# T1 written centred with its mean in a 129th column, z on ScalarE with one pointer

## The reference

```python
x = einsum('oc,bchw->bohw', inv(I - circulant(ricker(width, damp))), x)   # mixes the 128 channels
t = x as tokens                                                           # (16, 1024, 128)
n = layernorm(t)
Q, K, V = elu(n @ Wq.T) + 1, elu(n @ Wk.T) + 1, n @ Wv.T                  # 8 heads of 16
t = t + (causal linear attention of Q, K, V) @ W_out.T                    # call this t1
z = layernorm(t1)
g = mean over tokens of (relu(z @ gfc1.T + b) @ gfc2.T + b)               # one gate vector per batch
W1m, b1m, W2m, b2m = W1 + sum_e g[e] * tv_W1[e], ...                      # weights merged per batch
r = z + relu(z @ W1m.T + b1m) @ W2m.T + b2m
t = t1 + layernorm(r) * gain + bias                                       # t1 comes back here
```

## Time and profile before

| | us |
|---|---|
| runs | 747.09, 748.32, 747.53 |
| profiled execution, its own time | 749.55 |
| its span in the trace | 747.80 |
| TensorE busy | 692.5 (93%) |
| VectorE busy | 659.1 (88%) |
| ScalarE busy | 649.1 (87%) |
| GpSimd busy | 465.2 (62%) |

### The profile page before, as it was taken

How to read it: one execution, slowest core, us unless ns; L and a number is a source line. 1 busy time by engine, 2 the same in 40 slices (tenths; PEclk the granted TensorE clock), 3 DMA queues, 4 the chain that set the end, 5 groups by cost and what they waited for, 6 DMA issues and landing times. The chain is left out here.

```text
span 747.8 us, 38168 instructions
## 1 busy us (share of the span) xinstructions
PE 692.5 (93%) x12002; PEld 533.8 (71%) x12002; DVE 659.1 (88%) x2409; ACT 649.1 (87%) x1780; POOL 465.2 (62%) x790
## 2 busy tenths in 40 slices
PE   4898899999999999999999999888999998999993
PEld 2576677777777777777777777775777787777772
DVE  5697889999999999999999999768898977998983
ACT  4797989999999999999999999557888876888883
POOL 3686778888888888888888888421333321333333
PEclk9798999999999999999999999899999999999998
DMA  4757676666666666666666666410222211222221
GB/s 149 112 110 134 132 129 129 148 143 131 148 142 132 148 141 132 148 141 134 148 139 135 148 142 123 74 51 1 73 85 83 71 58 31 85 70 84 84 84 70
DMA packets 202485, 82.66 MB, mean 111 GB/s; under 512 B 176093, under 2 KB 189824, under 8 KB 202377
## 3 DMA queue, kind: packets, MB, share of 16 engines
q1 hardware_dynamic: 202440, 82.08, 48.3%
HBM read 22.79 MB, written 17.30 MB: 54 GB/s over the span
## 5 line engine op out<-in xcount | busy, mean ns | idle before, releaser
L892 DVE SCALAR_TENSOR_TENSOR scores_lo<-p_a,scores_hi 128x512 f16<-128x512 f32 x256 | 173.3, 683 | 1.7 <-ACT scores_hi L786 1.3
L786 ACT ACTIVATE scores_hi<-p_a 128x512 f16<-128x512 f32 x256 | 156.2, 611 | 9.3 <-PE p_a L623 9.3
L1010 POOL CAST qk_parts<-qk_f 128x512 f16<-128x512 f32 x128 | 78.0, 610 | 50.2 <-issue 24.9
L1442 POOL TENSOR_TENSOR ffn_rstd_shift<-ffn_rstd_shift,consts 128x4 f32<-128x4 f32 x32 | 36.5, 1142 | 109.1 <-DVE ffn_rstd_shift L1400 109.1
L984 POOL TENSOR_TENSOR stats<-stats,consts 128x2 f32<-128x2 f32 (+1 forms) x128 | 88.2, 689 | 17.9 <-DVE stats L925 13.1
L1224 PE MATMUL psb<-merged_W_of_batch,h_hi 128*128 128x128 f16 x512 | 94.5, 220 | 2.2 <-DVE h_lo L1378 1.5
L1378 DVE TENSOR_TENSOR h_lo<-h_f,h_hi 128x512 f16<-128x512 f32 x128 | 95.6, 786 | 1.1 <-ACT h_hi L1280 1.1
L1269 ACT ACTIVATE h_f<-psb,merged_b_of_batch 128x512 f32<-128x512 f32 x128 | 87.2, 709 | 10.3 <-PE psb L1205 8.6
L1225 PE MATMUL psb<-merged_W_of_batch,h_hi 128*128 128x128 f16 x512 | 94.2, 220 | 0.0
L1226 PE MATMUL psb<-merged_W_of_batch,h_lo 128*128 128x128 f16 x512 | 94.1, 220 | 0.0
L1016 POOL TENSOR_TENSOR qk_parts<-qk_f,qk_parts 128x256 f16<-128x256 f32 x128 | 85.9, 671 | 10.2
(11 more groups left out here) (215 smaller groups left out, 2697.5 us busy)
## 6 DMA issues: line engine op xcount, KB each, us to landing
x_f<-in_x SPq DMA_DIRECT2D x32, 256.0 KB, 3.2
t_rows<-t SPq DMA_DIRECT2D x64, 128.0 KB, 1.8
t_back<-t_rows SPq DMA_DIRECT2D x32, 256.0 KB, 2.6
out<-out_tile SPq DMA_DIRECT2D x32, 256.0 KB, 2.1
tv_share<-in_L_ffn_tv_W SPq DMA_DIRECT2D x32, 128.0 KB, 2.2
qkT_parts<-qk_parts SPq DMA_TRANSPOSE x128, 3.1
zT_hi_lo<-z_parts SPq DMA_TRANSPOSE x128, 2.3
merged_W<-in_L_ffn_W SPq DMA_DIRECT2D x2, 256.0 KB, 4.4
```

The lines of the kernel that those rows point to most:

```text
L786: nc.scalar.activation(ah[:, t % 2, cols], p_a[:, cols], ACT.Relu).then_inc(ahi_ready[eo], 1)
L892: nc.vector.scalar_tensor_tensor(al[:, t % 2, cols], p_a[:, cols], 0.0, ah[:, t % 2, cols], ALU.max, ALU.subtract).then_inc(alo_ready[eo], 1)
```

## The change

The weights that make t1 are centred, so that t1 comes out of `out_project` with mean 0 over the channels: block 4 of `w_in` is now the centred mix, and `w_outT` has each row's mean taken off. The mean itself comes out as one more column, the 129th, of the same four matmuls. `read_t1` copies 129 columns, the stores and loads carry them. `normalise` now is a copy with one pointer, z = t1 times one over the deviation; `shift2` is gone. In the second phase `add_up` puts the mean back: instead of one addition over 512 columns it is four scalar_tensor_tensor instructions of 128 columns, each adding t1 and the mean's column, read through a pointer. Setup computes the extra column and the centred weight. `conv` uses the centred mix as well. The lists of ScalarE, VectorE and GpSimd for the first phase are in another order; those of the second phase are not.

```diff
-SCALAR_ORDER = [("normalise", 10), ("split_x", 0), ("relu_qk", 2), ("read_t1", 7), ("gate_relu", 14),
-                ("exp_qk", 1), ("state_hi", 3), ("v_hi", 1), ("tv_hi", 0), ("scores_hi_0", 4), ("copy_out", 6),
+SCALAR_ORDER = [("relu_qk", 2), ("split_x", 0), ("normalise", 10), ("read_t1", 7), ("gate_relu", 14), ("tv_hi", 0),
+                ("exp_qk", 1), ("state_hi", 3), ("v_hi", 1), ("scores_hi_0", 4), ("copy_out", 6),
                 ("scores_hi_1", 4)]
-VECTOR_ORDER = [("shift2", 9), ("divide", 6), ("make_qk", 2), ("v_lo", 2), ("stats2", 7), ("stats1", 0),
...
+VECTOR_ORDER = [("make_qk", 2), ("divide", 6), ("v_lo", 2), ("stats2", 7), ("stats1", 0), ("mean_var1", 0),
...
-GPSIMD_ORDER = [("rsqrt", 1), ("z_hi", 10), ("split_x", 0), ("z_lo", 10), ("qk_hi", 2), ("qk_lo", 2),
+GPSIMD_ORDER = [("rsqrt", 1), ("split_x", 0), ("z_hi", 10), ("z_lo", 10), ("qk_hi", 2), ("qk_lo", 2),
                 ("last_rsqrt2", 8)]
...
-                    nc.vector.tensor_scalar(wbig[:, 0:C], pa[:, 1, 0:128], WSI, None, ALU.mult)
+                    nc.vector.tensor_scalar(wbig[:, 3 * C:4 * C], pa[:, 1, 128:256], WSI, None, ALU.mult)
                     link(nc.vector.tensor_copy(gfh[:, :], wsqT[:, 4, :]))
+                    nc.vector.scalar_tensor_tensor(wbig[:, 4 * C:4 * C + 1], pa[:, 1, 0:1], WSI, wbig[:, 3 * C:3 * C + 1],
+                                                   ALU.mult, ALU.subtract)
                     dve.wait_ge(s_wtc, 1)
-                    nc.vector.tensor_scalar(woT[:, :], wsqT[:, 3, :], WSI, None, ALU.mult)
-                    link(nc.vector.tensor_tensor(gfl[:, :], wsqT[:, 4, :], gfh[:, :], ALU.subtract))
+                    link(nc.vector.tensor_reduce(v[:, 15:16], wsqT[:, 3, :], AX.X, ALU.add))
+                    nc.vector.tensor_tensor(gfl[:, :], wsqT[:, 4, :], gfh[:, :], ALU.subtract)
+                    link(nc.vector.tensor_scalar(woT[:, C:C + 1], v[:, 15:16], WSI / C, None, ALU.mult))
+                    nc.vector.tensor_scalar(woT[:, 0:C], wsqT[:, 3, :], WSI, woT[:, C:C + 1], ALU.mult, ALU.subtract)
...
-                        o, cols = p_m1[:, 0:P], slice(j * P, (j + 1) * P)
-                        mm(o, xh[:, hf, cols], wh[:, 0:C], start=True, stop=False)
+                        o, cols = p_m1[:, 0:C + 1], slice(j * P, (j + 1) * P)
+                        mm(o, xh[:, hf, cols], wh[:, 3 * C:4 * C + 1], start=True, stop=False)
...
-                        nc.scalar.activation(yt[:, t, :], p_m1[:, 0:P], ACT.Copy, scale=1.0 / WSI).then_inc(t1_ready, 1)
+                        nc.scalar.activation(yt[:, t, :], p_m1[:, 0:C + 1], ACT.Copy, scale=1.0 / WSI).then_inc(t1_ready, 1)
...
-                        act.wait_ge(shift_ready, n + 1)
+                        act.wait_ge(rstd, n + 1 + PAIRED)
                         at_least(act, zlo_ready, n - 1)
-                        nc.scalar.activation(z_[:, t % 2, :], yt[:, t, :], ACT.Identity, bias=st2[:, (t + 3) % 4, SHIFT:SHIFT + 1],
-                                             scale=st2[:, (t + 3) % 4, RSTD:RSTD + 1]).then_inc(z_ready, 1)
+                        nc.scalar.activation(z_[:, t % 2, :], yt[:, t, 0:C], ACT.Copy, scale=st2[:, (t + 3) % 4, RSTD:RSTD + 1])\
+                            .then_inc(z_ready, 1)
...
-                        nc.vector.tensor_tensor(rn[:, hf, :, :], rn[:, hf, :, :], t1b[:, hf, :, :], ALU.add)\
-                            .then_inc(v_ready, 1)
+                        for j in range(HALF):
+                            last = nc.vector.scalar_tensor_tensor(rn[:, hf, j, :], t1b[:, hf, j, 0:C], t1b[:, hf, j, C:C + 1],
+                                                                  rn[:, hf, j, :], ALU.add, ALU.add)
+                        last.then_inc(v_ready, 1)
```

More of the change, by code:

```diff
@@ L43 @@
                 ("gate", 13), ("project", 0)]
-SCALAR_ORDER = [("normalise", 10), ("split_x", 0), ("relu_qk", 2), ("read_t1", 7), ("gate_relu", 14),
-                ("exp_qk", 1), ("state_hi", 3), ("v_hi", 1), ("tv_hi", 0), ("scores_hi_0", 4), ("copy_out", 6),
+SCALAR_ORDER = [("relu_qk", 2), ("split_x", 0), ("normalise", 10), ("read_t1", 7), ("gate_relu", 14), ("tv_hi", 0),
+                ("exp_qk", 1), ("state_hi", 3), ("v_hi", 1), ("scores_hi_0", 4), ("copy_out", 6),
                 ("scores_hi_1", 4)]
-VECTOR_ORDER = [("shift2", 9), ("divide", 6), ("make_qk", 2), ("v_lo", 2), ("stats2", 7), ("stats1", 0),
-                ("state_lo", 3), ("mean_var1", 0), ("mean_var2", 7), ("scores_lo_0", 4), ("denominator", 5),
-                ("scores_lo_1", 4), ("tv_lo", 1), ("invert", 5)]
-GPSIMD_ORDER = [("rsqrt", 1), ("z_hi", 10), ("split_x", 0), ("z_lo", 10), ("qk_hi", 2), ("qk_lo", 2),
+VECTOR_ORDER = [("make_qk", 2), ("divide", 6), ("v_lo", 2), ("stats2", 7), ("stats1", 0), ("mean_var1", 0),
+                ("mean_var2", 7), ("state_lo", 3), ("tv_lo", 1), ("scores_lo_0", 4), ("scores_lo_1", 4),
+                ("denominator", 5), ("invert", 5)]
+GPSIMD_ORDER = [("rsqrt", 1), ("split_x", 0), ("z_hi", 10), ("z_lo", 10), ("qk_hi", 2), ("qk_lo", 2),
                 ("last_rsqrt2", 8)]
@@ L146, in build @@
         delta2h = sb(top, "delta2_f16", [P, GB, FI], F16)
-        wh = sb(top, "w_in_hi", [P, 4 * C], F16)
-        wl = sb(top, "w_in_lo", [P, 4 * C], F16)
-        woT = sb(top, "w_outT", [P, C])
+        wh = sb(top, "w_in_hi", [P, 4 * C + 1], F16)
+        wl = sb(top, "w_in_lo", [P, 4 * C + 1], F16)
+        woT = sb(top, "w_outT", [P, C + 1])
         gfh = sb(top, "gate1_hi", [P, C], F16)
@@ L229, in build @@
             maskf = sb(su, "mask_factors", [P, 2 * P + P // 2])
-            wbig = sb(su, "w_in", [P, 4 * C])
+            wbig = sb(su, "w_in", [P, 4 * C + 1])
             cw = sb(su, "centred_inverse", [P, C])
@@ L447, in run @@
                     batch(stages, b, behind)
-            MEAN, VAR, RSTD, SHIFT = 9, 10, 11, 12
+            MEAN, VAR, RSTD = 9, 10, 11
             PAIRED = 7
@@ L566, in conv @@
                         o, cols = p_m1[:, 2 * P:3 * P], slice(j * P, (j + 1) * P)
-                        mm(o, xh[:, hf, cols], wh[:, 0:C], start=True, stop=False)
-                        mm(o, xh[:, hf, cols], wl[:, 0:C], start=False, stop=False)
-                        mm(o, xl[:, hf, cols], wh[:, 0:C], start=False, stop=True).then_inc(conv_done, 1)
+                        mm(o, xh[:, hf, cols], wh[:, 3 * C:4 * C], start=True, stop=False)
+                        mm(o, xh[:, hf, cols], wl[:, 3 * C:4 * C], start=False, stop=False)
+                        mm(o, xl[:, hf, cols], wh[:, 3 * C:4 * C], start=False, stop=True).then_inc(conv_done, 1)
                     def project(b, t):
@@ L966, in _ @@
                     run(dve, VECTOR_ORDER, {"tv_lo": tv_lo, "stats1": stats1, "mean_var1": mean_var1, "v_lo": v_lo,
-                        "make_qk": make_qk, "shift2": shift2, "state_lo": state_lo,
+                        "make_qk": make_qk, "state_lo": state_lo,
                         "scores_lo_0": scores_lo(0), "scores_lo_1": scores_lo(1), "denominator": denominator,
```

34 lines of the change are left out of this document (14 added, 20 removed).

## The result

The changed kernel takes 786.86 us (median of four runs, 782.17 to 788.84) against 747.92 us; the ratio is 1.0518, with a 95% interval of [1.0488, 1.0547]. The forecast was 752.0 us, with a range from 739 to 763. The sign was right, the size was not. The profiled execution spans 787.0 us against 747.8.

The account below looks back on a forecast made before the run. VectorE was taken to set the time in first-phase tiles without a share, a circle of 6.55 us the second phase. -9.9 + 0.3 + 13.6 + 0.5 = +4.5 us gave 752.0 us, range 739 to 763.

Parts of the forecast that it names:

- z (402 ns, 424 forecast): ScalarE's `normalise`, first phase: one pointer less saves 90 ns of 514, 11.5 us of ScalarE's time.
- the waits on `stats1` (0.38) and `denominator` (0.19): VectorE, first phase: 0.40 us from `stats1` to `mean_var1`, then `state_lo`; 0.19 us from `denominator` to `invert`.
- `tv_lo` (301 ns): VectorE, first phase: in its new place its stretch falls from 0.52 to about 0.1 us, near 0.4 us at most.
- the 129th column: Four matmuls and one ScalarE copy a column wider: +0.3 us, 1.3 us if all five were on one path.
- the whole second phase: Four adds in `add_up` lengthen a circle that hides nothing: 0.44 us a half-batch, +13.6 us, round 6.99 against 6.55.
- the choice: VectorE, first phase: new waits fill places where it already waits for other engines, 1.5 us a batch, without adding to them.
- The -9.9: First phase: a batch of 27.2 us against 27.8, so 16 x 0.62 us gained by VectorE.
- 26.3 and 27.2: VectorE's own work per first-phase batch in us, summed for the kernel before and for the changed one.
- third rival: The first phase gives nothing: new waits come on top of the old, or TensorE's share doesn't follow; 762 us, chance 0.16.
- a queue that was put at 0: SP's queue: stores of t1 grow from 1024 to 1032 bytes a row, nobody waits for DMA, so cost 0.
- VectorE sets the time in a tile without a share: First phase, tiles without task weights: VectorE's instructions follow without waits, 3.09 us from `make_qk` to `make_qk`.
- the moved `denominator`: VectorE, first phase: moved from between the two `scores_lo`, `invert` waits for it at once, +0.11 us a tile.

Follow-up runs that it names:

- e12: e9 with a constant 0.0 in place of the pointer in `add_up`, so t1's mean is not added back: 744.16 us.
- e9: e8 with the store of t1 issued by ScalarE in place of SyncE: 750.10 us.
- e8: The changed kernel with `state_lo`, `denominator` and `divide` moved back in VectorE's first-phase list, `tv_lo` alone staying moved: 759.44 us.
- e1: The changed kernel with the first-phase lists of ScalarE, VectorE (without `shift2`) and GpSimd all as before: 760.08 us.
- e2: The changed kernel with VectorE's first-phase list alone as before (without `shift2`): 760.47 us.
- e6: The changed kernel with `denominator` alone moved back, between the two `scores_lo`: 761.79 us.
- e3: The changed kernel with ScalarE's first-phase list alone as before: 786.56 us.
- e10: The changed kernel with the store of t1 issued by ScalarE in place of SyncE, nothing else: 787.33 us.
- e5: The changed kernel with `state_lo` alone moved back, between `stats1` and `mean_var1`: 774.66 us.
- e7: The changed kernel with `divide` alone moved back, ahead of `make_qk`: 780.18 us.
- e4: The changed kernel with GpSimd's first-phase list alone as before (`z_hi` ahead of `x_lo`): 784.93 us.
- e11: The kernel before the change with the store of t1 issued by ScalarE in place of SyncE, nothing else: 748.58 us.
- e15: The kernel before the change with one move alone, `denominator` behind both `scores_lo` and `tv_lo`: 751.08 us.

## Why the prediction was wrong

*Right:* z (402 ns, 424 forecast), the waits on `stats1` (0.38) and `denominator` (0.19), `tv_lo` (301 ns), the 129th column, and the whole second phase. The row of `v_lo` gave the price of an add with a pointer (0.26 each; 1.05 measured for four). The rule in the Trainium skill, "VectorE: DVE Perf Modes", section "The TRN2 errata", by which the forecast estimated 0.78, agrees with the four adds of e12 (0.81). It has no term for the pointer.

*The step that failed* is the choice: "I take it that the new waits fill these places and don't add to them". In the changed kernel VectorE's own row of a batch is 27.64 us (3.17 + 3 x 3.37 + 4 x 3.59, the last with `tv_lo`), and the batch without a drop 29.12: VectorE still waits 1.5 us, as before, so nearly all of the longer row (1.3 us by the same sum) came on top (1.2). The -9.9 set a sum without waits, 27.2, against a measured batch with them, 27.8. Like against like the forecast's own sums were 26.3 and 27.2, a loss of 0.9 a batch, 14 us in sixteen. Its third rival named this, but priced it at a gain of 0 and no loss.

*Behind that stand three things.* First, a queue that was put at 0 by DMA's share of 0.65: SyncE issues without a longer gap at 27.9 us a batch, and e9 shows for e8 that it holds the batch there, so that on these lists neither a lighter ScalarE nor a shorter VectorE gains anything (e1, e2, e8). The forecast's reading that VectorE sets the time in a tile without a share doesn't carry over to the batch. Second, the moved `denominator` was sized at 0.11 us and costs 0.25, and it lies ahead of `divide`, for which TensorE waits (5.0 us from 150 to 430 us; in e6 the view shows no such wait); taking this move back alone restores the first phase (e6). Third, the rows of the kernel before have no clock drop between tile 24 and tile 120, so none was in the sum; eight came, 12.0 us. The drops lie in the kernels in which TensorE idles once a batch for 0.55 us or more (the changed one 8, e3 6, e10 4, e5 3 of twelve batches), and one in e7, whose longest idle time is 0.41; e4 idles longer in sum (15.5 us of waits from 150 to 430 us against 10.9) but never over 0.39 at a time, and has none. That the long idle time brings the drop is suggested by this and not shown.

*What stays open.* In times the four moves don't add up: undone singly they give back 12 (`state_lo`), 25 (`denominator`) and 7 us (`divide`), these three undone together 27 (e8). In batches without a drop they nearly do: 0.5, 1.2 and -0.2 us against 1.2 together, where 27.9 is reached. But `denominator` moved alone in the kernel before costs 4 us. That fits a picture in which the latest of several limits counts (SyncE's queue at 27.9, VectorE's row with its waits below it before and above it after), but no run shows why the lengthening is taken up in the one kernel and not in the other. Nor is it shown why the same idle time of TensorE is followed by a drop of the clock in some batches and not in others, nor which of the two candidates holds e11 at 28.06.

## What to carry to other kernels

Add up a queue that issues DMAs like an engine: time from issue to issue, and the view of its waits. If it waits for nothing, it may be a bound, whatever share the DMA engines show; moving some of its issues elsewhere tells (9.3 us in e9), and it can gain nothing where another limit stands at the same height (e11). A small instruction between two that depend on each other can be free (`shift2` was), and taking it away or moving it exposes the wait; so the price of a move is read from both places, with the neighbours' times. A sum without waits is compared with a sum without waits, not with a measured batch. Where several engines stand at the same height, less work on one gains little, and more work on another can be taken up (e15: 1.0 us in the row, 0.32 in the batch) or cost nearly its full length (the changed kernel: 1.3 and 1.2), with falls of the clock besides.

## What the runs showed of the hardware

- Issuing a DMA that transposes held SyncE's queue 1.17 to 1.24 us, a plain one 0.34 to 0.39, with 0.2 to 0.3 us to the next (kernel before); on ScalarE the plain store's issue took 0.35 us beside running activations (e9).
- A scalar read through a pointer costs VectorE 60 ns on a scalar_tensor_tensor of 128 columns (1.05 us for four in the changed kernel, 0.81 in e12).
- A fall of TensorE's clock to the 1.2 GHz level made the batch in which it lay 1.5 us longer in the changed kernel, e3, e5 and e10, 5%, and 1.05 us in e7.
- `scores_lo` to `make_qk` through two 8-column instructions took 0.37 us behind the last of the large ones (272.16 to 272.53), against 0.07 + 0.11 = 0.18 for the two in e6, where one of them stands between the large ones.
